# The four stores of a block's count table, asked for by GpSimd instead of SyncE, in a two-layer graph network

## The reference

```
h = x @ W + b_W;  xi, xj = split(h, 2)
xji = (xj[src] + edge_attr @ W_e + b_We) / (in_degree[dst] + 1e-6)
x   = layernorm(x + xi + segment_sum(xji, dst))

h   = x @ W1;  deg counts the edges into a node and one self loop
out = segment_sum(h[src] / sqrt(deg[src] * deg[dst]), dst) + b1     # edges and self loops
y   = batch norm of out over the nodes, times gamma, plus beta;  y = y if y >= 0 else 0.01 * y
x   = layernorm(x + y)
```

## Time and profile before

| What | Value |
|---|---|
| Median of 3 runs | 932.84 us (927.0 to 935.95) |
| The profiled execution | 936.61 us, span 934.8 us |
| Mean granted TensorE clock | 0.989 of full speed |
| Busy share of the span | PE 94%, DVE 72%, ACT 48%, POOL 40% |
| Moved by DMA | 247.99 MB, mean 265 GB/s |
| Loop over the blocks | about 9 to 705 us of the span |
| Second layer from stored tables | about 705 to 900 us, then the last norm |

### The profile page before, as it was taken

One profiled execution on the slowest core, in us unless ns is written; L12 is line 12 of the kernel. 1 busy time (PEld: TensorE's weight loads), 2 busy tenths in 40 slices (PEclk: granted clock), 3 DMA queues, 4 the chain that ended last, 5 costly groups with the idle time before them and its releaser, 6 DMA issues.

```text
span 934.8 us, 30543 instructions
## 1 busy us (share of the span) xinstructions
PE 880.2 (94%) x12209; PEld 788.6 (84%) x12209; DVE 675.4 (72%) x1245; ACT 444.2 (48%) x970; POOL 370.1 (40%) x400
## 2 busy tenths in 40 slices
PE   5699989889999999999999999999999999999995
PEld 4688888779888998898999999999988888888874
DVE  7999998969989898888898989988832111112255
ACT  3855666566556656655565556565532000000025
POOL 4266554425455454444364455634431011111100
PEclk9799999999999999999999999999999999999998
DMA  8769799998888979777778788779767986778643
GB/s 283 244 199 347 296 332 309 329 295 270 276 257 304 287 232 303 247 228 220 261 235 285 205 234 250 278 222 292 215 205 295 367 347 266 278 258 323 250 159 128
DMA packets 104333, 247.99 MB, mean 265 GB/s; under 512 B 40710, under 2 KB 62810, under 8 KB 100474
## 3 DMA queue, kind: packets, MB, share of 16 engines
q1 hardware_dynamic: 102586, 242.69, 77.8%
q0 software_dynamic: 1600, 3.28, 1.4%
HBM read 187.08 MB, written 58.85 MB: 263 GB/s over the span
## 4 chain that ended last, share of the span: by engine, by line
PE 84%; DVE 6%; ACT 3%; issue 3%; DMA 3%; SPq 0%; ACTq 0%; DVEq 0%
PE x_ps L867 26%; PE pair_ps L944 17%; PE pair_ps L849 14%; PE e_ps L888 11%; PE x_ps L875 9%; PE j_ps L926 2%; ACT counts L1050 1%; DMA counts_kept<-counts 1%; DVE lo_oh L615 1%; PE j_ps L927 1%; DMA key_oh<-sums_z 1%; DVE key_oh L618 1%; PE pair_ps L953 1%; PE u_vps L1384 1%; DVE xsplit L673 1%
## 5 line engine op out<-in xcount | busy, mean ns | idle before, releaser
L1050 ACT CAST counts<-pair_ps 128x784 bf16<-128x784 f32 x391 | 315.0, 817 | 259.0 <-PE pair_ps L849 233.0
L867 PE MATMUL x_ps<-counts,xsplit 128*128 128x256 bf16 (+1 forms) x2450 | 305.3, 270 | 2.5 <-issue 2.5
L615 DVE TENSOR_TENSOR lo_oh<-counter,lo_t 128x2048 bf16<-128x2048 bf16 x196 | 246.0, 1255 | 58.7 <-PE pair_ps L849 58.6
L867 PEld LDWEIGHTS x_ps<-counts,xsplit 128*128 128x128 f16 x2450 | 221.2, 97 | 31.2 <-issue 9.8
L849 PE MATMUL pair_ps<-key_oh,lo_oh 128*128 128x100 bf16 x3128 | 208.6, 209 | 21.9 <-ACT counts L1050 13.4
L849 PEld LDWEIGHTS pair_ps<-key_oh,lo_oh 128*128 128x128 bf16 x3128 | 183.1, 98 | 36.0 <-issue 19.9
L618 DVE TENSOR_TENSOR key_oh<-counter,key_t 128x1600 bf16<-128x1600 bf16 x196 | 201.1, 1026 | 0.0
L888 PE MATMUL e_ps<-streams 128*32 128x128 f32 x3528 | 108.0, 274 | 1.9 <-issue 1.9
L875 PE MATMUL x_ps<-counts,zown 128*128 128x256 bf16 (+1 forms) x840 | 106.8, 270 | 2.7 <-issue 2.7
L888 PEld LDWEIGHTS e_ps<-streams 128*32 128x32 f32 x3528 | 94.1, 110 | 6.8 <-issue 3.0
L944 PE MATMUL pair_ps<-streams,zown 128*128 128x256 bf16 x878 | 99.0, 273 | 0.0
(11 more groups left out here) (171 smaller groups left out, 900.7 us busy)
## 6 DMA issues: line engine op xcount, KB each, us to landing
streams<-in_edge_attr SPq DMA_DIRECT2D x196, 576.0 KB
counts_kept<-counts SPq DMA_DIRECT2D x31, 384.0 KB
streams<-counts_kept SPq DMA_DIRECT2D x6, 1600.0 KB, 6.4
counts_kept<-counts SPq DMA_DIRECT2D x10, 768.0 KB
counts_kept<-counts SPq DMA_DIRECT2D x17, 448.0 KB
counts<-counts_kept SPq DMA_DIRECT2D x4, 1600.0 KB, 6.5
streams<-counts_kept SPq DMA_DIRECT2D x2, 3136.0 KB, 14.6
counts_kept<-counts SPq DMA_DIRECT2D x8, 704.0 KB
```

The source lines that it names most:

```text
L615: dv.tensor_tensor(lo_oh[:, ring, :, :, :].rearrange("p r w k t -> p (r w) k t"), counter[:, :, :].unsqueeze(1).to_broadcast([P, g, P, 2]) ...
L867: last = nc.tensor.matmul(x_ps[:, 0, 0:n], xsplit[:, q // 2, q % 2, :], by_hi[:, q // 2, :], start=(q == 0), stop=(q == 2 * HS - 1))
L1050: a.copy(out.rearrange("p h (g n) -> p h g n", g=2), pair_ps[at % 2][:, :, 0:4 * KW].rearrange("p g (n h) -> p h g n", h=HI)[:, 0:HS]).the ...
```

## The change

`keep_counts` moves from SP's stream to GpSimd's. The transfers, their sizes, the semaphore they raise and ACT's wait for it stay as they are. GpSimd asks for the stores of block b-1 in its turn for block b, behind the two gathers and ahead of `add_biases`; block 0 is no exception any more.

```
@@ SP
-            def keep_counts(k):
-                sp.wait_ge(S["pair_out"], first_slot(k) + slots(k))
-                for at, n in store_parts(k):
-                    sp.dma_start(scratch["counts"][k * P:(k + 1) * P, at:n], counts[k % 2][:, at:n])\
-                      .then_inc(counts_kept[k % 2], 16)
-
             def load_edges(b, g, starts):
                 ...
-                        if c == EG - 1:
-                            keep_counts(0)
                 ...
                     load_destinations(b, starts)
-                    if 2 <= b <= NB - 2:
-                        keep_counts(b - 1)
                     keep_inverse(b)
@@ GpSimd
+            def keep_counts(k):
+                pool.wait_ge(S["pair_out"], first_slot(k) + slots(k))
+                for at, n in store_parts(k):
+                    g.dma_start(scratch["counts"][k * P:(k + 1) * P, at:n], counts[k % 2][:, at:n])\
+                     .then_inc(counts_kept[k % 2], 16)
                 ...
                 if b + 2 < NB:
                     windows(b + 2)
+                if 1 <= b <= NB - 2:
+                    keep_counts(b - 1)
                 if b >= 1:
                     add_biases(b - 1)
```

## The result

The changed kernel is slower: 944.97 us as the median of four runs (943.74 to 946.73) against 931.24 us for the kernel before on the same chip (927.0 to 935.95). The ratio is 1.0167, with a 95% interval of 1.0136 to 1.0199. The profiled execution took 946.73 us, its span 944.9 us. The time lies in the range of the prediction (926 to 948 us), but 10 us above its number and on the slower side, to which it had given a chance of 0.24. The step of 13.7 us is also beyond the upper bound of its sum, 9.1 us: the range holds the time only by the 6 us that it had added for spread and a mild form of the first rival, so that it does is in part luck.

A forecast was written before the change was run, and what follows sets the result against it. The prediction took PE to bound the block loop. Its terms, 0 + 0 + 0 + 1.8 us, raised the median from 932.84 to 934.6 us, say 935 us, with a range of 926 to 948 us.

The forecast's parts named there:

- first rival: Stores late in each of 20 blocks from 4 on; with 1 us each, 953 us; chance 0.14.
- SyncE loses four requests: SyncE's stream: four requests a block go, its 5.8 us wait grows by as much; gain on the path 0.
- GpSimd gains 92 requests: GpSimd's turn: 1.87 us a request, 7.5 us for four, fitting into 12.4 us of waits; cost 0.
- GpSimd becomes the bound: Slower rival: from 3.1 us a request GpSimd's turn is too long; at 3.5 us, 970 us; chance 0.08.
- DVE beside the requests: DVE's one-hots beside GpSimd's requests aren't slowed: taken as 0, upper bound 8.6 us.
- Block 1: Table 0 lands at 78.9 us; ACT waits 7.1 us, PE stops 4.8 us and then lags 5.0 us.
- Block 3: Stores land at 125.4 us after a gather until 110.20 us; block 4 starts 1.0 to 2.6 us later, taken as 1.8.
- PE's lag doesn't add: At block 4: PE's 5.0 us lag, less 2.8 us of spare time, brings it to 124.2 us, or 127.0 without.
- Later blocks: Block 20: stores land at 592.1 us, ACT wants the buffer at 594.2 us; 2.1 us to spare, cost 0.
- nowhere later: Sign in the profile: ACT waits for stores at the starts of blocks 2 and 4 only.
- Stops of PE go: Faster rival: two queues ease PE's stops; 12 of 20.5 us idle could go, 921 us; chance 0.07.
- third rival: The faster rival, Stops of PE go: 12 of PE's 20.5 us idle could go, 921 us; chance 0.07.

The follow-up runs named there:

- e12: e5, with SyncE asking for edge group 0 only when the stores have landed; 924.79 us, ratio 0.9975 to the kernel before.
- e5: Changed kernel, with GpSimd asking for the stores in its idle time, between check_edges and shares; 929.75 us, ratio 1.0013 to the kernel before.
- e6: Kernel before, stores of tables 1 to 22 cut to 64 columns a transfer and table 0 read in place of each; 923.18 us, ratio 0.9958.
- run 100: Not a label of a run: the sentence says that in every run 100 packets of 16 KB are of a queue for instructions.
- e1: Changed kernel, with GpSimd asking for all stores earlier in its turn, ahead of the edge checks; 936.44 us, ratio 1.0082 to the kernel before.
- e2: Changed kernel, with SyncE waiting for the stores before it asks for edge group 1; 947.76 us, ratio 1.0213 to the kernel before.
- e3: Kernel before, SyncE's store requests held back behind edge group 0 and a wait for GpSimd's gathers, ahead of group 1; 953.39 us, ratio 1.0271.
- e4: Changed kernel, with only tables 0, 2 and 4 asked for early in GpSimd's turn, ahead of the edge checks; 940.48 us, ratio 1.0122.
- e9: Changed kernel, stores of tables 1 to 22 cut to 64 columns a transfer and table 0 read in place of each; 929.24 us, ratio 1.0011.
- e7: Kernel before, with SyncE asking for the stores ahead of the edge receivers instead of behind them; 924.27 us, ratio 0.9960.
- e10: e7 once more, in five rounds, against the kernel before; 927.57 us, ratio 0.9984.
- e8: The kernel before, unchanged, run once more for a second profile; 936.11 us.
- e11: Kernel before, with SyncE asking for the stores first in its turn, ahead of start_values and the edge receivers; 931.08 us, ratio 1.0024.

## Why the prediction was right and where it failed

From request to landing, table 2 (landing is the end of the wait for it):

| Kernel | Who asks | Asked for, us | Landed, us | Between |
|---|---|---|---|---|
| before | SyncE | 107.83 | 124.36 | 16.5 |
| changed | GpSimd | 117.22 | 135.13 | 17.9 |
| group 1 held back | GpSimd | 114.76 | 134.46 | 19.7 |
| late, on SyncE | SyncE | 121.12 | 137.11 | 16.0 |
| group 0 held back | GpSimd | 102.90 | 118.69 | 15.8 |

It is 16 to 20 us for this table, whoever asks. With the request at 117.22 us the row of before would have given 133.8 us, where 135.13 was measured; but the prediction had the request at 110.20 us, and from there the same row gives 126.7 us. So most of the error is in the time of the request and not in the way to landing.

The neighbours do count. Table 0 took 17.1 us in the changed kernel (63.21 to 80.34 us), 13.3 us with group 1 held back (64.28 to 77.56 us) and 10.3 us on SyncE's queue with group 1 behind it (68.69 to 78.95 us). Nor was table 2 alone in `e12`: from 102 to 116 us DMA moved 5.3 MB, of which the table is 3.1 MB, and group 1 of the block before had been asked for at 96.88 us.

- **SyncE loses four requests: 0.** Right. Its wait for new rows went from 5.8 us a block to 176.7/20 = 8.8 us, 3.0 us more, at the edge of the 3 to 4 us foreseen.
- **GpSimd gains 92 requests: 0.** Right in the cost, wrong in the price. A request took 0.57 us and not 1.87, so 2.2 us a turn and not 7.5. The gather was a poor nearest row, and even the lower bound of about 1 us was too high; GpSimd's two waits shrank from 12.4 to 181.9/23 + 84.6/25 = 11.3 us a turn and not to 5. The rival in which GpSimd becomes the bound had to have 3.1 us a request and is out.
- **DVE beside the requests: 0.** Right. A key one-hot that runs beside the four requests of block 2 (87.77 to 89.95 us) took 0.98 us, as beside a gather:

```profile
88.14 0.98 DVE L616 TENSOR_TENSOR key_oh<-counter,key_t 128x1600 bf16<-128x1600 bf16 x1
```

The rule weighed there, the Trainium skill, "SBUF — State Buffer", the box on DVE blocking DMA, doesn't show in these numbers: four requests took 2.2 us where that page's example gave an estimate of 19 us, and `e5` with them on GpSimd has the time of before. The box speaks of DVE's two-port modes, and no row here says that the one-hots run in one, so this is no evidence against it.
- **Block 1.** The mechanism was right and near in size: landed at 80.34 us (forecast 78.9), ACT's wait 8.34 us (7.1), PE's stop 7.27 us (4.8). ACT began block 3 at 104.38 us, 6.2 us later than before; I had 5.0 us of lag.
- **Block 3, the step that failed.** "PE's lag doesn't add", and the stores land at 125.4 us. I let PE's lag move ACT's wish for the buffer, and left GpSimd's gather at the 110.20 us of the old trace. But GpSimd's turn waits for DVE, and DVE, with its ring of six slots full, waits for PE, as a wait of DVE late in block 2 and GpSimd's first row of the turn for block 3 show:

```profile
100.55 1.23 DVE L613 TENSOR_TENSOR lo_oh<-counter,lo_t 128x2048 bf16<-128x2048 bf16 x1 [1.74 <-PE pair_ps L847]
```

```profile
104.59 0.22 POOL L471 TENSOR_SCALAR quot<-deg 128x2 f32<-128x2 f32 x1 [11.21 <-DVE junk L592]
```

The lag came through to the gather, which ended at 117.22 us, 7.0 us later. ACT's wish moved by 6.9 us, so the lag covered nothing. At block 3 it did cover: the request of table 1, at 87.77 us, had slipped by only 2.0 us and ACT's wish by 6.2 us, and there is no wait. The other 2.7 us are the way to landing, 17.9 us instead of 125.4 - 110.2 = 15.2. So block 4 paid 6.22 us, and block 6 the same again, 5.81 us. Where the sum has 1.8 us, the three stops of PE took 17.5 us, and the span grew by 10.1 us. Each stop also had its low clock, for which I had 1.5 us once.
- **Later blocks: 0.** About right in cost, wrong in form: ACT waits in blocks 8, 9, 10, 12, 17 and 19 too, which "nowhere later" denied, but for 1.8 us at most. These cost PE little; block 8 begins 13.3 us later than before, block 20 10.3 us.
- **Stops of PE go.** The third rival was put at 12 us and a chance of 0.07, and part of it happened unseen: the stops without a releaser fell from 10.1 to 1.9 us. The account of PE's waits from 60 to 700 us is 24.6 - 8.1 = 16.5 us more for ACT's casts, 8.2 us less without a releaser and 1.6 us less for others, so 6.7 us; the spans differ by 10.1 us. The low clock can hold the other 3.4 us: PE's busy time times the missing part of the clock, in windows of 1 us, is 5.9 us against 1.4 us before.

Against `e6`, the kernel before in that comparison loses 7 us by the medians (930.2 and 923.18 us) and 4 us by the ratio; in its profile the stops without a releaser are 8.7 us more than in `e6`. The changed kernel loses those stops and has the stops for the stores in their place.

What the stops without a releaser are, the packed traces tell in part. They hold the start and the end of each DMA packet, and in every run 100 packets of 16 KB are of a queue that the page calls one for instructions:

```profile
q8 instruction: 100, 1.64, 0.7%
```

All 14 profiles together have 32 stops of PE of 0.6 us or more without a releaser from 60 to 700 us. Of these, 27 end 1.2 to 1.6 us after such a packet has landed, as the one of 3.71 us in `e1` does (1.4 us); for a moment picked at random the chance of that is 0.05. So PE was very likely waiting for its instructions. No run changed when they come, and that this queue is PE's is inferred.

What stays open: why five of the 32 don't fit, why those stops nearly vanish wherever PE also stops for ACT (0.8 to 2.0 us in `e2`, `e3`, `e4`, `e9` and the changed kernel), and why `e1`, 5 to 6 us earlier than `e5` in blocks 2 to 4, has the most of them. They need the bytes of the stores (`e6`), and those 3.71 us fell where DMA moved 391 to 410 GB/s.

## What to carry to other kernels

Before moving a transfer, read from the trace how long it is under way from its request to the wait that it ends, and what else was under way with it, and shift that whole time; a sum of bytes over the full rate was 2.7 us short here. Then, which was worth more, ask what sets the time of its new neighbours in the stream: if their engine hangs on the engine that the late transfer stops, the request slips with the stop and the lag gives no cover. It is the place in the turn that counts and not the engine: the same four requests on the same engine cost 14 us behind the gathers and nothing that shows in the idle time ahead of `shares`.

## What was not expected of the hardware

A request for a plain store took GpSimd 0.57 us. SyncE took 0.9 to 1.1 us in the earlier trace rows, and 0.53 to 1.06 us over the 20 rows of the kernel before that hold four of them.

The stops of PE without a releaser, summed from 60 to 700 us, go with the time of the profiled execution (`e7` and `e10` are the same kernel, `e8` is the kernel before; the kernels that stop for ACT are left out):

| Kernel | Stops without a releaser, us | Time, us |
|---|---|---|
| `e6` (bytes gone) | 1.4 | 922.41 |
| `e12` | 0.9 | 923.14 |
| `e10` | 2.2 | 924.86 |
| `e7` | 5.7 | 929.48 |
| `e11` | 7.5 | 932.17 |
| `e5` | 7.7 | 932.19 |
| `e8` | 9.5 | 936.11 |
| before | 10.1 | 936.61 |
| `e1` | 11.8 | 936.62 |

Within one kernel `e7` and `e10` alone bear it out: 3.5 us more of these stops and 4.6 us more time. That the spread of the kernel before, 923 to 936 us, is these stops too isn't shown, since both of its profiles lie near 936 us. Its rows are to be read with their own time beside the median.
